# A chunked state-space scan on one Trainium2 core: history laid out by state, three groups a step, blocks of 12 steps, and a warm-up of 20 steps

## What is computed

```python
x_sub = x[:, ::2]                                  # 2048 tokens
x_sub = x_sub * rsqrt(mean(x_sub**2) + EPS) * g_norm
x_proj, gate = split(x_sub @ w_in.T + b_in, 2)
def step(h, xt):                                   # h: [256 channels, 64 states]
    h = tanh(h * A + xt[:, :, None] * Bm)
    y = h @ c_sum + Dv * xt                        # sum over the 64 states
    return (h, y)
out = scan(step, 0, x_proj) * silu(gate)
out = out @ w_out.T + b_out                        # each row is used for two tokens
```

## Time and profile before

| | us |
|---|---|
| Median of 3 runs | 4241.61 |
| Lowest and highest | 4234.35, 4251.05 |
| The profiled execution | 4239.84 |
| Its span in the trace | 4238.0 |
| PE busy in it | 3707.6 (87%) |
| DVE busy | 3012.5 (71%) |
| ACT busy | 1988.4 (47%) |
| Pool busy | 1108.8 (26%) |
| `project_in` and the loading of weights | 0 to 64 |
| `scan_chunks` | 64 to 1092.5 |
| `project_out`, first issue | 1094.5 |

### The profile page before, as it was taken

The page is one execution under the profiler, slowest core; times in us unless marked ns, Lnnn a source line. Parts: engine busy times, 40 slices in busy tenths (PEclk is TensorE's granted clock), DMA queues, the critical chain, the costliest instruction groups (busy, mean ns, idle before and its releaser), DMA issues. The chain is left out here.

```text
span 4238.0 us, 71202 instructions
## 1 busy us (share of the span) xinstructions
PE 3707.6 (87%) x26410; PEld 2713.2 (64%) x26410; DVE 3012.5 (71%) x4742; ACT 1988.4 (47%) x3791; POOL 1108.8 (26%) x1129
## 2 busy tenths in 40 slices
PE   3199999999908998388999999999999984799997
PEld 1199999999607887374455555555555533688886
DVE  6977777777413443658888888888888804788888
ACT  2433333333104444123577777777777771233333
POOL 2755665555062111600001111121111021000000
PEclk7599999999859999597799999999999997899999
DMA  4000000000022221473020202112020000000001
GB/s 165 0 1 0 0 0 0 0 0 0 3 105 80 79 82 58 120 206 49 7 38 17 43 12 43 29 31 42 13 44 15 9 18 11 16 11 11 15 11 40
DMA packets 85092, 150.87 MB, mean 36 GB/s; under 512 B 16512, under 2 KB 53269, under 8 KB 83138
## 3 DMA queue, kind: packets, MB, share of 16 engines
q1 hardware_dynamic: 64514, 104.12, 10.2%
q0 software_dynamic: 19584, 42.14, 3.2%
q10 hardware_dynamic: 768, 1.57, 0.3%
HBM read 90.60 MB, written 57.41 MB: 35 GB/s over the span
## 5 line engine op out<-in xcount | busy, mean ns | idle before, releaser
L1693 DVE TENSOR_REDUCE row_max<-psum 128x2 f32<-128x1024 f32 (+2 forms) x1152 | 1250.7, 1132 | 226.7 <-PE psum L1567 174.0
L1646 ACT ACTIVATE probs_T<-psum 128x512 f32<-128x512 f32 (+3 forms) x2304 | 1121.4, 565 | 373.6 <-PE psum L1591 294.1
L357 PE MATMUL psum<-h_hist,csum_diag 128*128 128x128 f32 x4096 | 899.1, 397 | 131.2 <-ACT h_hist L341 131.2
L357 PEld LDWEIGHTS psum<-h_hist,csum_diag 128*128 128x128 f32 x4096 | 845.5, 207 | 184.5 <-issue 131.4
L1591 PE MATMUL psum<-q_rows,k_rows 50*128 50x512 f32 (+3 forms) x2304 | 775.8, 443 | 10.3 <-ACT probs_T L1646 9.7
L322 POOL TENSOR_TENSOR x_times_b<-x_slab,B_sb 128x512 f32<-128x512 f32 x576 | 611.1, 1063 | 435.9 <-DVE psum L271 360.1
L1567 PE MATMUL psum<-k_rows,q_rows 48*128 48x512 f32 (+3 forms) x2304 | 647.5, 455 | 41.0 <-DVE row_max L1693 24.6
L341 ACT ACTIVATE h_hist<-psum 128x512 f32<-128x512 f32 x576 | 344.4, 598 | 657.2 <-DVE psum L271 657.2
L1611 PE MATMUL psum<-probs_T,v_all 128*17 128x256 f32 (+1 forms) x8704 | 606.4, 381 | 0.7 <-issue 0.6
L1591 PEld LDWEIGHTS psum<-q_rows,k_rows 50*128 50x128 f32 x2304 | 367.9, 189 | 322.6 <-ACT probs_T L1646 269.4
L271 DVE TENSOR_TENSOR psum<-psum,x_times_b 128x512 f32<-128x512 f32 x576 | 403.2, 700 | 62.5 <-DVE psum L267 3.5
(11 more groups left out here) (212 smaller groups left out, 3108.3 us busy)
## 6 DMA issues: line engine op xcount, KB each, us to landing
w_raw<-in_w SPq DMA_DIRECT2D x16, 1024.0 KB, 8.2
qk_rows<-qk_split SPq DMA_DIRECT2D x64, 256.0 KB, 3.0
q_rows<-qk_rows SPq DMA_DIRECT2D x42, 256.0 KB, 11.6
k_rows<-qk_rows SPq DMA_DIRECT2D x42, 256.0 KB, 16.9
inbox<-zeros SPq DMA_DIRECT2D x8, 1024.0 KB, 10.5
xe_sb<-inbox SPq DMA_DIRECT2D x8, 1024.0 KB, 5.9
outbox<-ye_sb POOLq DMA_DIRECT2D x8, 1024.0 KB, 10.2
o_raw<-o_acc POOLq DMA_DIRECT2D x64, 128.0 KB, 2.0
```

The source lines that it names most:

```text
L357: last = pe.matmul(ps[:, 1 + j, 0:BL * DH * CHUNKS], diag[:, s, :], hist[:, j, :, :, :].rearrange("p t h (c s) -> p (t h) c s", s=NS)[:, : ...
L1646: act.activation(pt[:, u % RING_P, j, o:CH], ps[:, S_BANKS + at_item % RING_ST, o:CH], ACT.Exp, scale=SCALE).then_inc(taken, 1)
L1693: dve.tensor_reduce(mx[:, n % 4, heads[0]:heads[-1] + 1, QT * c + i % QT, mm], ps[:, banks, 0:width], AX.X, ALU.max).then_inc(maxed, 1)
```

## The change

Seven things change, all in the scan and around it.

1. The history, and all that is computed from it, lies as (state, chunk) in place of (chunk, state). The 8 chunks of one state are neighbours. In line 280 A is repeated along the innermost axis (8 chunks). The matmul's moving operand is made of runs of 8 floats.
2. A step is worked in three groups in place of two: states 0 to 47 of half 0, the same of half 1, and states 48 to 63 of both halves (384, 384 and 256 elements). DVE issues the three multiplies of a step ahead of its three adds.
3. Blocks have 12 steps, so the history holds 24, and a matmul has 192 columns. 22 of 23 blocks are summed by PE, in place of 32 of 36. To make room, `diag` uses `k.stream`.
4. The load of x into `k.stream` therefore moves from `load_scan_weights` to `project_out`, in 8 transfers of 512 KB; w_out is issued behind the first, b_out and wg behind the last.
5. Pool goes through its operands with the chunk outside and the state inside. x is repeated and B read in order, and the product is written in steps of 8 floats.
6. The slab copy moves from DVE to ACT, in the middle of the block before; it waits for Pool to have finished the block before that one.
7. `WARM` is 20 in place of 32: 276 steps in place of 288.

The core of the diff:

```diff
-WARM = 32
-BL = 8
+WARM = 20
+BL = 12
...
-            sp.dma_start(k.stream[:, :, :].rearrange("p (i j) c -> p i (j c)", j=2),
-                         a["x"].rearrange("(i p j) c -> p i (j c)", p=P, j=2)).then_inc(k.x_loaded, 16)
...
+    CUT = 48
+    GROUPS = ((slice(0, 1), slice(0, CUT)), (slice(1, 2), slice(0, CUT)), (slice(0, 2), slice(CUT, NS)))
...
-        diag = sb("csum_diag", [P, NS, P])
+        diag = k.stream[:, :, :].rearrange("p n c -> p (n c)").rearrange("p (s q) -> p s q", s=NS)
...
+        def part(tile, i):
+            halves, states = GROUPS[i]
+            return tile.rearrange("p h (s c) -> p h s c", s=NS)[:, halves, states, :]
+
+        def over_chunks(tile, i):
+            halves, states = GROUPS[i]
+            shape = [P, halves.stop - halves.start, states.stop - states.start, CHUNKS]
+            return tile[:, halves, states].unsqueeze(3).to_broadcast(shape)
+
+        def u(i):
+
+            if i < DH:
+                return ps[:, 5 + i, 0:CUT * CHUNKS].rearrange("p (h s c) -> p h s c", h=1, c=CHUNKS)
+            return ps[:, 7, 0:DH * (NS - CUT) * CHUNKS].rearrange("p (h s c) -> p h s c", h=DH, c=CHUNKS)
...
             def steps(B, slot):
                 for t in range(BL):
                     prev = hist[:, slot, t - 1] if t else hist[:, 1 - slot, BL - 1]
-                    for g in range(DH):
-                        n = 2 * BL * B + 2 * t + g
-                        if isinstance(n, int) and n < 2:
+                    for i in range(NG):
+                        n = NG * BL * B + NG * t + i
+                        if isinstance(n, int) and n < NG:
                             dve.wait_ge(h_zero, 1)
                         else:
-                            dve.wait_ge(h_ready, n - 1)
-                        dve.tensor_tensor(ha[:, g, :].rearrange("p (c s) -> p c s", s=NS), prev[:, g, :].rearrange("p (c s) -> p c s", s=NS),
-                                          ps[:, 0, g * NS:(g + 1) * NS].unsqueeze(1).to_broadcast([P, CHUNKS, NS]), ALU.mult).then_inc(ha_ready, 1)
+                            dve.wait_ge(h_ready, n - NG + 1)
+                        dve.tensor_tensor(part(ha, i), part(prev, i), over_chunks(A, i), ALU.mult).then_inc(ha_ready, 1)
+                    for i in range(NG):
+                        n = NG * BL * B + NG * t + i
                         dve.wait_ge(xb_ready, n + 1)
                         dve.wait_ge(ha_ready, n + 1)
-                        dve.tensor_tensor(u[:, g, :], ha[:, g, :], xb[:, t % RING_X, g, :], ALU.add).then_inc(u_ready, 1)
-
-            def take_y(m, bank):
-
-                dve.wait_ge(y_done, m + 1)
+                        dve.tensor_tensor(u(i), part(ha, i), part(xb[:, t % RING_X], i), ALU.add).then_inc(u_ready, 1)
...
                 last.then_inc(y_taken, 1)
 
-            slab(0, ring(0))
-            for B in range(NWARM):
-                slab(B + 1, ring(B + 1))
...
+            for B in range(NLOOP):
+                steps(B, B % 2)
+                if B > B0:
+                    if B == B0 + 1:
+                        dve.wait_ge(k.x_saved, 16)
+                    take_y(B - 1, (B - 1) % 2, T0 if B == B0 + 1 else 0)
+            with dve.Fori(0, (NB - NLOOP) // 2) as i:
+                for j in range(2):
+                    steps(2 * i + NLOOP + j, (NLOOP + j) % 2)
+                    take_y(2 * i + NLOOP + j - 1, (NLOOP + j - 1) % 2)
...
-                    for g in range(DH):
-                        n = 2 * BL * B + 2 * t + g
-                        if not isinstance(n, int) or n >= 2 * RING_X:
-                            pool.wait_ge(u_ready, n - 2 * RING_X + 1)
-                        pool.tensor_tensor(xb[:, t % RING_X, g, :].rearrange("p (c s) -> p c s", s=NS),
-                                           xs[:, slot, g, :, t].unsqueeze(2).to_broadcast([P, CHUNKS, NS]),
-                                           k.B[:, g, :].unsqueeze(1).to_broadcast([P, CHUNKS, NS]), ALU.mult).then_inc(xb_ready, 1)
-
+                    for i in range(NG):
+                        n = NG * BL * B + NG * t + i
+                        if not isinstance(n, int) or n >= NG * RING_X:
+                            pool.wait_ge(u_ready, n - NG * RING_X + 1)
+                        halves, states = GROUPS[i]
+                        out = part(xb[:, t % RING_X], i).rearrange("p h s c -> p h c s")
+                        shape = list(out.shape)
+                        x = xs[:, slot, halves, :, t].unsqueeze(3).to_broadcast(shape)
+                        b = k.B[:, halves, states].unsqueeze(2).to_broadcast(shape)
+                        pool.tensor_tensor(out, x, b, ALU.mult).then_inc(xb_ready, 1)
...
+            def slab(B, slot):
+
+                src = k.xpT[:, :, bass.ds(B * BL, TP)].rearrange("p h (c l) -> p h c l", l=LEN)[:, :, :, 0:BL]
+                if not isinstance(B, int) or B >= 2:
+                    act.wait_ge(xb_ready, NG * BL * (B - 1))
+                act.activation(xs[:, slot, :, :, :], src, ACT.Copy).then_inc(xs_ready, 1)
+
             def steps(B, slot):
                 for t in range(BL):
-                    for g in range(DH):
-                        n = 2 * BL * B + 2 * t + g
+                    if t == BL // 2 and not (isinstance(B, int) and B == NB - 1):
+                        slab(B + 1, 1 - slot)
+                    for i in range(NG):
+                        n = NG * BL * B + NG * t + i
                         act.wait_ge(u_ready, n + 1)
-                        if isinstance(B, int) and B == NWARM - 1 and t == BL - 1:
-                            act.activation(warm[:, g, :], u[:, g, :], ACT.Tanh).then_inc(warm_kept, 1)
-                        act.activation(hist[:, slot, t, g, :], u[:, g, :], ACT.Tanh).then_inc(h_ready, 1)
...
+            def outputs(B, j):
+                pe.wait_ge(h_ready, NG * BL * (B + 1))
                 for s in range(NS):
                     last = pe.matmul(ps[:, 1 + j, 0:BL * DH * CHUNKS], diag[:, s, :],
-                                     hist[:, j, :, :, :].rearrange("p t h (c s) -> p (t h) c s", s=NS)[:, :, :, s],
+                                     hist[:, j, :, :, :].rearrange("p t h (s c) -> p (t h) s c", s=NS)[:, :, s, :],
                                      start=(s == 0), stop=(s == NS - 1))
...
         @block.sync
         def _(sp):
-            sp.dma_start(w[:, :, :], a["w_out_T"].rearrange("(h p) e -> p h e", p=P)).then_inc(loaded, 16)
+            for g in range(NG_LN):
+                rows = slice(g * LNG // 2, (g + 1) * LNG // 2)
+                sp.dma_start(k.stream[:, :, :].rearrange("p (i j) c -> p i (j c)", j=2)[:, rows, :],
+                             a["x"].rearrange("(i p j) c -> p i (j c)", p=P, j=2)[:, rows, :]).then_inc(x_in[g], 16)
+                if g == 0:
+                    sp.dma_start(w[:, :, :], a["w_out_T"].rearrange("(h p) e -> p h e", p=P)).then_inc(loaded, 16)
             sp.dma_start(bo[:, :], a["b_out"].rearrange("(o e) -> o e", o=1)).then_inc(loaded, 16)
             sp.dma_start(wg[:, :, :], a["wg"].rearrange("(h p) e -> p h e", p=P)).then_inc(wg_in, 16)
...
-            dve.wait_ge(k.x_loaded, 16)
             for i in range(NPAIR):
+                if i * 2 % LNG == 0:
+                    dve.wait_ge(x_in[i * 2 // LNG], 16)
                 dve.wait_ge(projected, i + 1)
```

More of the change, by code:

```diff
@@ L332, in _ @@
+            for B in range(3):
+                products(B, B % 2)
+            with pool.Fori(0, (NB - 3) // 2) as i:
+                for j in range(2):
+                    products(2 * i + 3 + j, (3 + j) % 2)
         @block.scalar
         def _(act):
+            def slab(B, slot):
[3 more added lines that the diff above has]
+                act.activation(xs[:, slot, :, :, :], src, ACT.Copy).then_inc(xs_ready, 1)
@@ L343, in _ @@
-            for B in range(NWARM + 2):
-                steps(B, ring(B))
-            with act.Fori(1, NMAIN // 2) as i:
+                        if isinstance(B, int) and B * BL + t == WARM - 1:
+                            act.activation(part(warm, i), u(i), ACT.Tanh).then_inc(warm_kept, 1)
+                        act.activation(part(hist[:, slot, t], i), u(i), ACT.Tanh).then_inc(h_ready, 1)
+            slab(0, 0)
+            for B in range(NLOOP):
+                if B >= B0 + 2:
+                    act.wait_ge(y_done, B - B0 - 1)
+                steps(B, B % 2)
```

81 lines of the change are left out of this document (33 added, 48 removed).

## The result

| | Before | After |
|---|---|---|
| Median, us | 4237.98 (4 runs) | 3970.73 (4 runs) |
| Lowest and highest | 4229.99, 4251.05 | 3958.41, 3977.26 |
| The profiled execution and its span | 4239.84, 4238.0 | 3958.41, 3956.8 |

The ratio of the times is 0.9368, with a 95% interval from 0.9337 to 0.9398. The forecast was 3987, the range 3965 to 4135: faster, inside the range, and 16 us longer than the median.

The account below looks back on a forecast made before the run. PE's output sums, 32 blocks of 28.0 us, were taken to bound the scan, with DVE next. The profiled 4239.8 less 267.2 for the scan, plus 12.5 for project_out, gave 3985.1, by the median 3987 us; range 3965 to 4135.

Parts of the forecast that it names:

- Start of the steps: Start of the scan: steps begin at 77.4 us as before, after the diagonal on DVE; Pool's head start saves 0.4 of waiting.
- 276 steps: Scan on DVE: 276 steps in place of 288, at 2.56 us each, 706.6 us in all.
- End of a block, 21 times: Scan on DVE: the two adds of a finished block and the loop's turn cost 0.6 us in 21 blocks, 12.6.
- Last tanh, PE's tail, test of the seams: End of the scan: 0.7 us for the last tanh, 27 for PE's last block (23 to 31), 1 for the seams.
- Later start of PE in `project_out`: Start of project_out: b_out and wg queue behind x, so PE starts 16 us after the first issue, 12.5 later.
- The straight line: PE's output sums: a line through 0.117 us (128 columns) and 0.245 (256) gives 0.181 us a record for 192.
- The repeated operand in PSUM: DVE's multiplies: repeating A from PSUM costs nothing; the rival, chance 0.05, has it cost 0.67 us a step, 4171 us in all.
- DVE's step: Scan on DVE: multiplies ahead of adds save 0.18 us waits; a step takes 2.56 us against 2.80, range 2.50 to 3.06.
- ACT's loop: ScalarE's tanhs within a step: they return before DVE's next multiplies, hidden with 0.16 us to spare.
- the rival: Pool's products in the scan: scattered writes add 0.93 ns an element, 3.18 us a step, Pool bounds, 4133 us; chance 0.27.
- the step on Pool: Pool's products in the scan: 1.885 ns an element and 98 ns fixed give 2.22 us a step, if scattered writes are free.
- Slower: Scan on Pool: scattered writes cost more than any row shows, from 3.57 us a step the gain no longer pays; chance 0.05.

## Why the prediction was right

It was right in its mechanism: PE leaves the path, DVE takes it, and a later start of `project_out` gives a little back. The sum by its terms (us):

| Term | Predicted | Measured | Difference |
|---|---|---|---|
| Start of the steps | 77.4 | 79.6 | +2.2 |
| 276 steps | 2.56 each | 2.52 each | -11 |
| End of a block, 21 times | 0.60 | 0.46 | -3 |
| Last tanh, PE's tail, test of the seams | 28.7 | 23.8 | -4.9 |
| Scan ends | 825.3 | 808.9 | -16.4 |
| Later start of PE in `project_out` | +12.5 | +11.8 | -0.7 |

These differences make 17.1 us. The profiled execution took 3958.4 where the sum gave 3985.1 for it, 26.7 less. Nearly all of the other 9.6 lies behind PE's first matmul of `project_out` (3140.1 us from there to the end before, 3130.8 after), where no gain was forecast and no other stage was changed: that part of the miss is within the spread between executions.

*PE.* The straight line gave 0.181 us a record for 192 columns; it is 0.179 over all, and 0.176 in the last block. The upper end, 0.219, is out. I chose the middle, 25.6 us a block, for want of a row; the line was better than the caution. That it was so close is partly luck, since the mean is made of two rates. After the pause of 8.12 us in front of the last block:

```profile
785.70:787.00 1.30, 1.30 (x4) 1.30 (x5) 1.27 (x3) 0.00 (x0) 0.00 (x0) 0.50 0.02 6
787.00:789.00 2.00, 2.00 (x9) 2.00 (x8) 0.96 (x1) 0.00 (x0) 0.00 (x0) 0.54 0.00 0
789.00:795.00 6.00, 6.00 (x39) 6.00 (x38) 0.00 (x0) 0.00 (x0) 0.00 (x0) 1.00 0.00 0
```

At a granted clock of 0.50 records start 0.32 us apart, nine of them, and then at 1.00 every 0.163. The slow ones cost nine times 0.157, which is the 1.4 that the prediction had added for them. The dense stream before stood at 1.00 from 300 to 500 us. In the blocks ahead the lower clock costs nothing, since PE waits for DVE there anyway; only in the last block is it on the path.

*The repeated operand in PSUM* was taken at no cost from a row with an operand from SBUF. It holds: 550 ns with it and 553 without.

*DVE's step.* Starts stand 0.465 us apart for 384 elements and 0.331 for 256, where I had 0.472 and 0.334. The miss is 1.5%, and the reason for the multiplies' going first stands: in turn, the step is 3.13 where 3.06 was expected.

*ACT's loop* was said to have 0.16 us to spare. In after the first tanh ends at 303.75 + 0.49 = 304.24, 0.18 ahead of its multiply. With two groups nothing is spare and DVE waits, so a small reserve was the right reading.

*Pool.* This step was the least certain, with a chance of 0.27 for the rival, and was right in its result but not in its number. The product of 384 takes 898 ns, not 821. Two things are in that. The scattered write isn't quite free (0.13 ns an element in the products of 512). And the fixed part was too small: with the scattered write the products take 660, 898 and 1133 ns for 256, 384 and 512 elements (the last in the run with two groups), so 1.85 ns an element and 187 fixed, where I had taken 98 from two memsets. With 187 fixed a dense product of 384 would take an estimated 844. That the step on Pool came out at 2.27 us for 2.22 is partly luck, since the three durations (2.46) overlap. 898 is close to 821 and far from 1178, and Pool stays under DVE's step by 0.25 us. How near that is the run with the chunk inside shows: 122 ns more a product and Pool is the bound.

*The start of the scan* has two misses that nearly cancel. I had the diagonal at its old 12.5 us. It took 18.9, since Pool, now ahead of DVE by four steps, works beside it, and these copies can't run while it does: +6.4. I had counted Pool's head start as a gain of 0.4. Against that, the scan's memset began 4.2 us earlier (59.96 for 64.12). Of these, 2.7 were there before anything had changed: the first load of `load_scan_weights` is issued at 54.16 us for 56.85, and in the other runs of this layout between 53.64 and 57.42. That part is luck. The other 1.5 us come from the load that left: from this first issue to the memset are 7.27 us before and 5.80 after, and the variants of after have 5.7 to 5.8 too. With the 4 MB of x no longer in the queue ahead of it, SP's issue of the save of x_proj takes 0.47 us where it took 4.11, and the barrier behind it opens sooner. Before, and after:

```profile
59.32 4.11 SPq L200 DMA_DIRECT2D x_proj<-xpT  x1
64.12 0.91 DVE L248 MEMSET h_hist<- 128x1024 f32 x1 [2.08 <-PEq L186]
```

```profile
56.12 0.47 SPq L197 DMA_DIRECT2D x_proj<-xpT  x1
59.96 0.91 DVE L262 MEMSET h_hist<- 128x1024 f32 x1 [0.56 <-PEq L186]
```

I had moved the load to its new place and costed it there, but not what its leaving frees, 1.5 us. The larger slip is the diagonal: I took Pool's head start as a gain, and it cost 6.4.

*The later start of `project_out`* went as argued: everything behind x in the queue waits for x, 15.2 us for 16. The run with the small transfers first shows that it was the order in the queue.

*Slower* was never near: it needed 3.57 us a step.

Of the scan's 284 us, the runs tell these shares, each as the loss in the stage when that part is taken back (they overlap, so they don't add up): the layout 252, multiplies ahead of adds 169, the slab copy on ACT 31, the shorter warm-up 30, Pool's operands 26, the third group 8. The blocks of 12 steps weren't tried alone.

## What to carry to other kernels

Read the spacing of one engine's records for each stage before asking which engine is busy. A matmul whose fp32 operand is gathered element by element pays for it in every column, and turning the layout, if the other engines can bear it, moves the bound. Then order the next engine's instructions so that none reads the result of the one right ahead of it. When a large transfer moves, look at both ends: what it now stands in front of, and what it no longer does. When an engine gets a head start, look at what shares its access to memory.

## What the runs showed of the hardware

- PE's fp32 records: 0.130 us for 128 columns side by side, 0.179 for 192, but 0.219 and 0.326 with the floats 64 apart. At the higher clock alone, records side by side start 0.112 and 0.163 us apart, so the scattered read costs a factor of two there; at the lower clock they start 0.213 and 0.32 apart, as the scattered ones do at the higher.
- After a pause of 8.12 us on PE the last block began at a granted clock of 0.50; the stream without pauses before stood at 1.00 from 300 to 500 us.
- DVE's copies with a scalar from SBUF to SBUF can't run beside Pool's products: 915 ns beside them and 272 without (in the first kernel after), and slab copies at 1000 ns for 223 when DVE no longer waits (the run with the layout alone). DVE's multiplies and adds, which have an operand in PSUM, take 550 ns for 384 while Pool is busy for 89% of the time.
- Pool's product in fp32 pays about 0.13 ns an element for writing 8 floats apart (1130 ns for 1063 with 512), and some 0.5 for reading one operand in wide steps (1020 ns for 384 elements, against an estimated 821 to 844).
- DVE's instruction that reads the PSUM result of the one right ahead starts 0.656 us behind it with 384 elements, an independent one 0.465.
- SP's issue of a transfer took 4.11 us right behind a transfer of 4 MB, and 0.47 without it.
- Gaps of about 2.6 us on DVE ahead of the copy in every second block of the loop, in the run with the slab copy there, are left without a cause.
